# Part of a VectorE subtraction moved to GpSimd in a two-layer graph network

## The reference

```
h = relu(layernorm(x))
e = leaky_relu(sj[:, None, :] + si[:, :, None] + ab)      # scores from h @ Wv + bv
T = adj * exp(e), rows divided by their sum
x = x + relu(h Wk0 + (T h) Wk1 + (T T h) Wk2 + biases)    # layer 0
h = relu(layernorm(x))
Ah = adj + I;  dh = rsqrt(rowsum(Ah))
x = x + relu(dh * (Ah @ (dh * h)) W + bias)               # layer 1
```

## Time and profile before

| | |
|---|---|
| median of three runs | 839.0 us |
| the profiled execution, and its span | 840.16 us, 838.4 us |
| TensorE matmul busy | 797.6 us, 95% |
| VectorE busy | 636.2 us, 76% |
| ScalarE busy | 515.6 us, 62% |
| GpSimd busy | 126.1 us, 15% |
| TensorE's granted clock | 0.994 of full speed |
| `a_lo` on VectorE | 128 instructions, 84.5 us, 686 ns each |

### The profile page before, as it was taken

How to read it: one execution, slowest core, us unless ns; L and a number is a source line. 1 busy time by engine, 2 the same in 40 slices (tenths; PEclk the granted TensorE clock), 3 DMA queues, 4 the chain that set the end, 5 groups by cost and what they waited for, 6 DMA issues and landing times.

```text
span 838.4 us, 15964 instructions
## 1 busy us (share of the span) xinstructions
PE 797.6 (95%) x6140; PEld 765.2 (91%) x6140; DVE 636.2 (76%) x1528; ACT 515.6 (62%) x997; POOL 126.1 (15%) x119
## 2 busy tenths in 40 slices
PE   4859999999999999999999999999999999999998
PEld 4749899998999999998999989999899999999998
DVE  4475687876879678796788868797787967886666
ACT  2695575666756576575756757566665757667232
POOL 1003111031101302022010311003020130102200
PEclk9988999999999999999999999999999999999999
DMA  5535441682517625284435835177151852347503
GB/s 188 181 121 167 147 134 57 218 284 65 187 35 251 222 79 174 72 299 133 138 114 162 291 114 162 34 246 251 63 190 47 284 185 67 123 128 239 175 12 102
DMA packets 65276, 128.71 MB, mean 154 GB/s; under 512 B 6320, under 2 KB 32304, under 8 KB 65200
## 3 DMA queue, kind: packets, MB, share of 16 engines
q1 hardware_dynamic: 54768, 93.86, 34.0%
q10 hardware_dynamic: 10432, 33.82, 12.8%
HBM read 119.28 MB, written 8.39 MB: 152 GB/s over the span
## 4 chain that ended last, share of the span: by engine, by line
PE 85%; DVE 5%; ACT 5%; DMA 2%; issue 2%; SPq 0%; ACTq 0%; DVEq 0%
PE acc L990 21%; PE acc L992 20%; PE acc L991 20%; PE da L860 12%; PE db L860 6%; PE tp L852 3%; ACT tg_e L378 2%; DMA a_raw<-adj_t_dram 2%; DVE ht_lo L589 1%; ACT ht_hi L338 1%; PE acc L880 1%; DMA h<-x_dram 1%; ACT t_hi L392 1%; DVE a_lo L639 1%; DVE h L570 0%
## 5 line engine op out<-in xcount | busy, mean ns | idle before, releaser
L990 PE MATMUL acc<-g_hi,t_hi 128*128 128x256 f32 (+1 forms) x1024 | 293.0, 286 | 3.0 <-issue 3.0
L992 PE MATMUL acc<-g_hi,t_lo 128*128 128x256 f32 (+1 forms) x1024 | 290.0, 283 | 0.0
L991 PE MATMUL acc<-g_lo,t_hi 128*128 128x256 f32 x1024 | 288.6, 282 | 0.0
L990 PEld LDWEIGHTS acc<-g_hi,t_hi 128*128 128x128 f32 x1024 | 194.0, 189 | 3.2 <-issue 3.2
L991 PEld LDWEIGHTS acc<-g_lo,t_hi 128*128 128x128 f32 x1024 | 194.3, 190 | 0.0
L992 PEld LDWEIGHTS acc<-g_hi,t_lo 128*128 128x128 f32 x1024 | 194.2, 190 | 0.0
L990 PE MATMUL acc<-g_hi,a_hi 128*128 128x256 f32 x512 | 147.1, 287 | 2.0 <-DVE a_lo L639 1.6
L991 PE MATMUL acc<-g_lo,a_hi 128*128 128x256 f32 x512 | 144.1, 281 | 0.0
L992 PE MATMUL acc<-g_hi,a_lo 128*128 128x256 f32 x512 | 144.1, 281 | 0.0
L378 ACT ACTIVATE tg_e<-si,sij 128x256 f32<-128x256 f32 x256 | 109.4, 501 | 12.8 <-DVE t_lo L633 10.2
L314 POOL TENSOR_TENSOR g_lo<-g_tmp,g_hi 128x256 fp32r<-128x256 f32 x64 | 57.9, 905 | 376.7 <-ACT g_hi L434 376.7
(11 more groups left out here) (108 smaller groups left out, 1474.1 us busy)
## 6 DMA issues: line engine op xcount, KB each, us to landing
tg_a<-adj_t_dram ACTq DMA_DIRECT2D x64, 512.0 KB, 4.2
a_raw<-adj_dram SPq DMA_DIRECT2D x64, 512.0 KB, 4.9
a_raw<-adj_t_dram SPq DMA_DIRECT2D x64, 512.0 KB, 4.5
x_res<-x_dram SPq DMA_DIRECT2D x64, 128.0 KB, 3.2
out_dram<-o_tile SPq DMA_DIRECT2D x64, 128.0 KB, 2.6
h<-x_dram SPq DMA_DIRECT2D x7, 1024.0 KB, 5.4
h<-x_dram SPq DMA_DIRECT2D x4, 256.0 KB, 4.9
p<-wk_dram SPq DMA_DIRECT2D x1, 768.0 KB, 7.8
```

The lines of the kernel that those rows point to most:

```text
L990: nc.tensor.matmul(acc[:, s, 0:n], l_hi, r_hi, start=(jt == 0), stop=False)
L991: nc.tensor.matmul(acc[:, s, 0:D], l_hi, r_lo, start=False, stop=False)
L992: ins = nc.tensor.matmul(acc[:, s, 0:n], l_lo, r_hi, start=False, stop=(jt == NT - 1))
```

## The change

The first-half low parts of chunks 4 to 7 of every batch are computed by GpSimd in place of VectorE: 4 of the 16 halves of a batch, 32 instructions in all. They stand at the end of GpSimd's work for a batch, behind the last power for the layer-1 norm, and wait for ScalarE's rounding of the half as VectorE's did. On VectorE they are left out at the steps 1 to 4, and the second half of chunk 3 stays at step 0. As `a_ready[0]` can now be behind `a_ready[1]`, SyncE waits for both before it loads into a slot of `a_raw`.

```diff
@@ rows(b, tiles), load_chunk(b, i) on SyncE
-                        sp.wait_ge(a_ready[1], b * NT + NT - RS + t + 1)
+                        for h in range(2):
+                            sp.wait_ge(a_ready[h], b * NT + NT - RS + t + 1)
...
-                    sp.wait_ge(a_ready[1], b * NT + i - RS + 1 + NT)
+                    for h in range(2):
+                        sp.wait_ge(a_ready[h], b * NT + i - RS + 1 + NT)
@@ GpSimd
+            def a_split(b, i):
+
+                pool.wait_ge(a_hi_done[0], b * NT + i + 1)
+                nc.gpsimd.tensor_tensor(a_half(a_lo, i, 0), a_raw[:, i % RS, 0:N // 2], a_half(a_hi, i, 0).bitcast(F32),
+                                        ALU.subtract).then_inc(a_ready[0], 1)
...
                     power(rstd1, ve1, ve1_ready, b * NG + g + 1, rstd1_ready, slice(2 * g, 2 * g + 2))
+                for i in range(4, NT):
+                    a_split(b, i)
@@ VectorE, batch, the loop of Z
-                    if i == 1:
-                        a_low(b, *A_FIRST[1])
-                    if i in A_THEN:
-                        a_low(b, *A_THEN[i])
+                    if i == 0:
+                        a_low(b, *A_THEN[0])
```

## The result

| | before | after |
|---|---|---|
| median of five runs each, same series | 839.71 us (838.85 to 840.81) | 843.99 us (842.14 to 845.15) |
| ratio, 95% interval | | 1.005 [1.0033, 1.0067] |
| the profiled execution, and its span | 840.16 us, 838.4 us | 842.14 us, 840.3 us |
| TensorE's granted clock | 0.994 | 0.994 |
| VectorE `a_lo` | 128 instructions, 686 ns each | 96, 764 ns each |

The change makes the kernel slower by 0.5%, or 4.3 us in this series. A later series timed it again: 844.69 against 839.58 us, ratio 1.0062 [1.0045, 1.0079].

A forecast was written before the change was run, and what follows sets the result against it. TensorE bounds the kernel, paced by VectorE in each last product; delays of 0.2, 0, 0.25, 0.85, 0.5, 0.75 and 0.7 us over seven batches give +3.3 us, from 839.0 to 842.3 us. Range 836.3 to 846, the forecast's own 841 to 845.

The forecast's parts named there:

- the hold of the second half of chunk 5: Last product, batch 3: GpSimd's chunk 6 goes first after VectorE's product; this half ends at 454.75, not 453.69.
- the sum: Chunk 6 starts 9.5 us after t_lo (9.75 in batch 2); later starts over batches 0 to 6 give +3.3 us.
- Length of the instruction: GpSimd's 512-column subtraction takes 0.74 + 0.54 = 1.28 us, between ends of 0.74 and 1.48.
- Who waits for whom: GpSimd waits out VectorE's two-SBUF-input instruction, enters before the next queued one, and ends 1.15 us after the first.
- the shorter hold that the sum used: Each GpSimd meeting on VectorE priced at 1.15 us, not the skill page's 1.28 us for the whole instruction.
- Its term: Batch 2 in the sum: chunk 6's transfer comes 0.3 us after the diagonal, so 9.75 us, a difference of 0.25.
- VectorE's backlog in the next batch: Next batch's first product: low parts needed only from chunk 4, 11 us in; priced at nothing, uncovered up to 1 us a batch.
- Chunk 7: End of the last product: later transfer and GpSimd's part still in time, with 0.2 to 0.4 us left; no cost.
- A: Rival: GpSimd's reads do not hold VectorE's subtractions; 2 to 4.5 us of hitches go, 834.5 to 837 us; chance 0.20.
- B: Rival: VectorE's queued a_lo goes first at the product's end; no change, 838 to 839.5 us; chance 0.22.
- C: Rival: GpSimd's subtraction takes 1.48 us or more and chunk 7's margins are used up; 846 to 848 us; chance 0.08.
- the 5 us of hitches: TensorE's late starts at chunks 4 to 7 of batches 0 to 6, about 5 us, the most relief of VectorE can bring.

The follow-up runs named there:

- experiment 1: Changed kernel with only chunk 6's first half on GpSimd, chunks 4, 5 and 7 back on VectorE: 845.25 us against 840.61 before, ratio 1.0053.
- the repeat: The changed kernel, unaltered, timed and profiled once more: 844.69 us against 839.58 before, ratio 1.0062.
- experiment 2: Changed kernel with chunks 4, 5 and 7 on GpSimd, chunk 6's first half on VectorE ahead of z_tmp 3: 843.37 us against 840.61 before, ratio 1.004.
- experiments 4 and 10: Changed kernel, GpSimd's four subtractions a batch replaced by three zero-filling memsets each (4: 836.36 us against 840.61) or a bare signal (10: 835.41 against 839.58).
- experiment 9: Kernel before the change with the loads of chunks 6 and 7 ahead of the stores of o_tile 1 and 2: 834.01 us against 839.58, ratio 0.9935.
- experiment 10: Changed kernel where GpSimd only waits and signals, the four low parts not computed: 835.41 us against 839.58 before, ratio 0.9949.
- experiment 3: Kernel before the change plus four GpSimd subtractions a batch of constant weights into an unread tile: 853.98 us against 840.61, ratio 1.016.
- experiment 7: Changed kernel, loads of chunks 6 and 7 ahead of o_tile 1 and 2's stores, chunk 5's second half ahead of VectorE's product: 840.77 us against 839.54 before.

## Why the prediction was right

The median came out at 843.99 us, 1.7 us above the 842.3 forecast and inside the forecast's own range of 841 to 845; the difference to before was +4.3 us where +3.3 was forecast. The mechanism, the hold of the second half of chunk 5, is the one that was forecast. That the sum is so near is in part luck: it is too high for the last product and leaves out a cost in the next batch. The steps of batch 3, in us after the start of t_lo (446.84 before, 445.46 after):

| step | predicted | measured |
|---|---|---|
| diagonal of chunk 5, held, ends | 2.56 | 2.51 |
| o_tile 2, held, ends | 4.91 | 4.81 |
| GpSimd arrives in the product for chunk 6 | 5.86 | 5.74 |
| second half of chunk 5 ends | 7.91 | 7.86 |
| TensorE goes on | 8.02 | 7.91 |
| chunk 6 starts on TensorE | 9.50 | 9.44 |
| diagonal of chunk 7 starts | 9.86 | 9.67 |

- **Length of the instruction.** 1.29 us by itself against 1.28: the fixed 0.74 plus the 0.54 by which the earlier trace rows saw VectorE held. Of its two ends, 0.74 and 1.48, the middle held.
- **Who waits for whom.** GpSimd's chunk 6 ended 452.77, 1.16 us after the product's end (451.61), against 1.15. The sightings in the earlier trace rows were enough, also the thin one of a power slipping between two back-to-back instructions; experiment 1 shows the same hand-over by itself.
- **What grows is not the whole instruction.** The held instructions lost 0.84 to 1.10 us of a GpSimd instruction of 1.29. The Trainium skill, page SBUF — State Buffer, section "SBUF: two separate sides", has the one that starts first keep the shared pair of ports for its whole instruction; the row of the held `a_lo` (1.79 instead of 0.69) shows 1.10 of 1.29, so the shorter hold that the sum used fits better.
- **The sum, at the place it was made for.** From t_lo to chunk 6 on TensorE the changed kernel takes 9.42 to 9.49 us in batches 0 to 6, forecast 9.5 (9.75 in batch 2). Against before that is +0.15, -0.05, -0.04, +0.79, +0.40, +0.71, +0.66: +2.6 us, where the prediction's steps gave +3.3. Of the 2.6 another 0.5 comes back, since the slower step behind chunk 6's late start (0.07 to 0.08 us a batch) has gone with it. So the last product costs +2.1 us (+2.6 in the repeat), and the sum was too high there, most of all in batch 2. Its term assumed that the transfer of chunk 6 would again come 0.3 us after the diagonal, and in the changed kernel that diagonal (351.19) had no idle time before it. How much of that transfer's lateness varies from run to run was not measured by itself.
- **VectorE's backlog in the next batch, priced at nothing.** This is the term that was wrong. The prediction looked at the low parts of the later units, which come in time, but not at the normalised `h` that TensorE transposes between chunks 6 and 7 of U: +0.7 us in the profile shown and +1.0 in the repeat, and +3.1 in experiment 2. By periods the whole is +3.07 and +3.80 us.
- **What the medians add.** +4.3 and +5.1 us in the two series, against +3.1 and +3.8 in the periods of one profile each. The two profiles of the changed kernel differ by 2.4 us in the start, which the change doesn't touch. Whether the start explains the medians is open.
- **Chunk 7.** Priced at nothing, and nothing was lost there in the profile shown (less than 0.1 us; 0.3 us in the repeat). But the cover was the wait at chunk 5, as experiment 2 showed, and not slack that the kernel had.
- **The rivals.** A (no hold) is refuted by the durations. Its price, 834.5 to 837 us, is what the relief brings where nothing is held: with no reads on GpSimd the time is 836.4 and 835.4 us (experiments 4 and 10). B (VectorE first at the hand-over) is refuted by the product and the `a_lo` behind it, which takes 1.77 to 1.79 us in all of batches 0 to 6. C (1.48 us) was not seen.

What the prediction did not ask is why VectorE was late at all. It took the 5 us of hitches as the most that relief could bring, and that number is right (the last products are 5.4 us shorter in sum in experiment 9 and 5.2 in experiment 10); but early loads remove all of them as well, by one edit on SyncE's queue.

## What to carry to other kernels

Before work is moved from VectorE to GpSimd, write down which VectorE instructions of that stage read two SBUF operands, and give each GpSimd subtraction that meets one about its own length as a cost to VectorE; the saving must be longer than that (here 0.84 to 1.10 us of hold against 0.60 us of relief). Look for the one instruction on the giving engine that has no slack, since one meeting there cost as much as all four (experiment 1). Follow the backlog into the next stage, to everything that the stage takes from that engine. And before an engine is relieved, look at what it waits for: here the idle time ahead of the diagonals named a transfer, and issuing that transfer before a store gave 0.65%, no less than free relief of the engine (0.51%).

## What the runs showed of the hardware that was not expected

- Three memsets of 1.37 us in all on GpSimd left VectorE's o_tile at 0.42 us, while one subtraction of 1.29 us made it 1.27.
- z_tmp, which reads PSUM and one SBUF tensor, stayed at 0.47 us beside GpSimd's subtraction at 448.70, in the same profile in which the next instruction, with two SBUF tensors, took 1.27. In experiment 3 it ran wholly inside one: z_tmp at 454.32 took 0.47 us, GpSimd's subtraction lasted from 453.99 to 455.55, and the o_tile behind took 1.00 instead of 0.43.
- A GpSimd instruction that waits in VectorE's 1.22 us product goes before the VectorE instruction queued behind it, whose own record still starts on time (451.53) and carries the hold as duration. The hold doesn't stand in VectorE's idle time, so a table of waits can't show it; mean durations do.
- TensorE's first matmul after such a wait is recorded with 0.36 to 0.39 us instead of 0.28, and the next one comes later than the usual 0.12 us behind it: 0.19 to 0.20 us at the first half of a chunk (before, and experiment 7), 0.22 to 0.23 at the second half (after). Each wait costs 0.07 to 0.11 us more than its lateness.
